# Whole-tile transfers for the residual, the result and x1's transposed copy in a one-core transformer layer

## What is computed

```
x1  = x + attention(layernorm(x)) @ Wo + bo          # one head, width 256
n   = layernorm(x1)
y   = relu(n @ up)^2 @ down                          # 1024 -> 2048 -> 1024
      + ((n @ fc1) @ expert * s) @ fc2               # s: sum of the two largest gate logits of the row
out = x1 + (layernorm(y) * gamma + beta)
```

## Time and profile before

| | |
|---|---|
| median of 3 runs | 2341.21 us (2341.16 to 2341.37) |
| the profiled execution, its own time | 2336.48 us |
| its span, first to last instruction | 2334.7 us |
| TensorE busy | 99% of the span |
| DMA traffic | 578.19 MB, 248 GB/s on average |

### The profile page before, as it was taken

How to read it: one execution, slowest core, us unless ns; L and a number is a source line. 1 busy time by engine, 2 the same in 40 slices (tenths; PEclk the granted TensorE clock), 3 DMA queues, 4 the chain that set the end, 5 groups by cost and what they waited for, 6 DMA issues and landing times.

```text
span 2334.7 us, 27253 instructions
## 1 busy us (share of the span) xinstructions
PE 2308.8 (99%) x10888; PEld 1940.2 (83%) x10888; DVE 1575.8 (67%) x1758; ACT 788.9 (34%) x875; POOL 292.9 (13%) x574
## 2 busy tenths in 40 slices
PE   9999999999999999999999999999999999999997
PEld 8988987888888878888888888888888888888886
DVE  7777658887988874598763378774249877334447
ACT  4433336666555433321221231213132122123210
POOL 3111000000223200033100023210003220000002
PEclk9999999999999999999999999999999999999999
DMA  8899854432334699889996678897668999667865
GB/s 305 334 357 367 290 193 139 169 126 79 129 111 128 222 325 324 295 279 334 329 307 202 192 272 299 311 347 250 195 218 274 323 338 308 207 192 208 243 204 181
DMA packets 232271, 578.19 MB, mean 248 GB/s; under 512 B 26320, under 2 KB 80208, under 8 KB 231760
## 3 DMA queue, kind: packets, MB, share of 16 engines
q1 hardware_dynamic: 150768, 440.90, 57.7%
q10 hardware_dynamic: 81376, 135.55, 15.8%
HBM read 420.91 MB, written 151.26 MB: 245 GB/s over the span
## 4 chain that ended last, share of the span: by engine, by line
PE 87%; DVE 6%; DMA 4%; ACT 1%; POOL 1%; issue 1%; SPq 0%; ACTq 0%; DVEq 0%; POOLq 0%
PE psum L114 86%; DMA wu_s<-QR0a 2%; DMA QR0a<-in_upfc_dram 1%; PE psum L354 1%; DVE QR0a L102 1%; DVE mx L102 1%; DVE PL L102 0%; DVE st L188 0%; DVE HB L102 0%; SPq L95 0%; DVE acc L102 0%; ACT SA L99 0%; ACT ATT L99 0%; POOL rA L102 0%; DVE ZR L108 0%
## 5 line engine op out<-in xcount | busy, mean ns | idle before, releaser
L102 DVE TENSOR_TENSOR HB<-HB,psum 128x1024 f32<-128x1024 f32 x140 | 169.2, 1218 | 302.1 <-PE psum L114 302.1
L99 ACT ACTIVATE HB<-HB 128x1024 f32<-128x1024 f32 x128 | 135.8, 1061 | 334.0 <-DVE HB L102 331.9
L105 POOL TENSOR_SCALAR veA<-mvA 128x1 f32<-128x1 f32 x32 | 31.6, 987 | 1279.5 <-DVE mvA L191 1279.5
L114 PE MATMUL psum<-XS1h,WR 128*128 128x512 f32 x560 | 174.8, 390 | 2.8 <-DMA WR<-wu_s 1.6
L114 PE MATMUL psum<-XS2h,WR 128*128 128x512 f32 x560 | 174.2, 390 | 2.0 <-DVE XS2l L102 2.0
L114 PE MATMUL psum<-XS0h,WR 128*128 128x512 f32 x560 | 175.4, 390 | 0.0
L114 PE MATMUL psum<-XS3h,WR 128*128 128x512 f32 x560 | 174.0, 389 | 0.0
L114 PEld LDWEIGHTS psum<-XS1h,WR 128*128 128x128 f32 x560 | 105.1, 188 | 25.4 <-DMA WR<-wu_s 2.3
L114 PEld LDWEIGHTS psum<-XS2h,WR 128*128 128x128 f32 x560 | 105.1, 188 | 24.1 <-issue 2.4
L114 PEld LDWEIGHTS psum<-XS0h,WR 128*128 128x128 f32 x560 | 105.2, 188 | 21.7
L114 PEld LDWEIGHTS psum<-XS3h,WR 128*128 128x128 f32 x560 | 105.1, 188 | 21.7
(11 more groups left out here) (326 smaller groups left out, 5874.7 us busy)
## 6 DMA issues: line engine op xcount, KB each, us to landing
WR<-wu_s SPq DMA_DIRECT2D x280, 512.0 KB, 4.3
WR<-wd_s SPq DMA_DIRECT2D x280, 512.0 KB, 4.8
att_s<-ATT ACTq DMA_DIRECT2D x32, 516.0 KB, 3.0
RAW<-in_x_dram SPq DMA_DIRECT2D x32, 512.0 KB, 8.5
RES<-x1b_s SPq DMA_DIRECT2D x128, 128.0 KB, 5.1
out_dram<-ZR ACTq DMA_DIRECT2D x112, 128.0 KB, 4.8
xT_s<-XT SPq DMA_DIRECT2D x24, 512.0 KB, 7.3
HB<-xT_s SPq DMA_DIRECT2D x12, 1024.0 KB, 8.2
```

Of the source, the lines that this page charges most:

```text
L99: return act.put(lambda e: e.activation(o, i, f, **kw), *toks)
L102: return (q or dve).put(lambda e: e.tensor_tensor(o, a, b, op=op), *toks)
L105: return (q or dve).put(lambda e: e.tensor_scalar(o, a, s1, s2, op0=op0, op1=op1), *toks)
L114: return pe.put(lambda e: e.matmul(o, w, m, start=start, stop=stop, **kw), *toks, sig=sig)
```

## The change

Three kinds of transfer get 128 partitions each. A task `xt(g)` stores piece m = g of all 128 partitions in place of all four pieces of 32 partitions; the number of these stores stays 24, of 512 KB each. A residual tile is one load in place of four, a result tile one store in place of four, and half a tile of the last block one store in place of four (the first half on ACT, the second on SP). ZR becomes [128, 4 tiles, 2 halves, 512], so that the halves of a result row lie side by side and a store's pieces are 4 KB in place of 2 KB. On the DRAM side each of these transfers now is a pattern of 4 blocks x 32 rows x 4 KB (2 KB in the last block).

```diff
-                src = T2[32 * g:32 * g + 32].rearrange("p m k t r -> p m (k t r)")
-                xt_st[t] = dma(xT_s[t, g].rearrange("(m c) n -> c m n", m=4), src, "xt", ln2_tr[t, 3])
+                src = T2[:, g].rearrange("p k t r -> p (k t r)")
+                xt_st[t] = dma(xT_s[t].rearrange("g (m c) n -> m g c n", m=4)[g], src, "xt", ln2_tr[t, 3])
...
-    ZR = [at("ZR0", [128, 2, 4, 512], F32, 188.125), at("ZR1", [128, 2, 4, 512], F32, 204.125)]
+    ZR = [at("ZR0", [128, 4, 2, 512], F32, 188.125), at("ZR1", [128, 4, 2, 512], F32, 204.125)]
...
-    def parts(s, r, g):
-
-        for i in range(4):
-            n = 512 * (2 * s + r) + 128 * i + 32 * g
-            yield slice(32 * i, 32 * i + 32), slice(n, n + 32)
+    def tile_rows(ap, s, r, g):
+
+        b = 512 * (2 * s + r)
+        return ap[b:b + 512].rearrange("(i g e) n -> g i e n", i=4, g=4)[g]
...
-        for ps, rs in parts(s, r, tt):
-            res_ld[s, r, tt] = dma(RES[i][ps].rearrange("p a n -> p (a n)"), x1b_s[rs], f"res{i}",
-                                   *(x1b_st[2 * s + r, q] for q in range(4)), *res_free.get(i, ()), *toks)
+        res_ld[s, r, tt] = dma(RES[i][:, :, :].rearrange("p a n -> p (a n)"), tile_rows(x1b_s, s, r, tt), f"res{i}",
+                               *(x1b_st[2 * s + r, q] for q in range(4)), *res_free.get(i, ()), *toks)
...
-        for ps, rs in parts(s, r, tt):
-            t = dma(out[rs].rearrange("p (a n) -> p a n", a=2), ZR[r][ps, :, tt, :], f"zo{r}{tt}", fin[s, r, tt], q=act)
-        z_free[r, tt] = (t,)
+        z_free[r, tt] = (dma(tile_rows(out, s, r, tt), ZR[r][:, tt].rearrange("p a n -> p (a n)"), f"zo{r}{tt}", fin[s, r, tt], q=act),)
...
-        for n, (ps, rs) in enumerate(parts(3, 1, tt)):
-            dma(out[rs, cs], ZR[1][ps, c, tt, :], f"zo{tt}{n // 2}", k, q=(act, sp)[n // 2])
+        dma(tile_rows(out, 3, 1, tt)[:, :, cs], ZR[1][:, tt, c, :], f"zo{tt}{c}", k, q=(act, sp)[c])
```

More of the change, by code:

```diff
@@ L1388, in z_evac @@
     def z_evac(s, p, ts_, b, k):
-        ZA, ZB, ZD, ZC = (ZR[r][:, c, ts_, :] for r in range(2) for c in range(2))
+        ZA, ZB, ZD, ZC = (ZR[r][:, ts_, c, :] for r in range(2) for c in range(2))
         tiles = range(ts_.start, ts_.stop)
@@ L1462, in z_stat @@
     def z_stat(s, r, tt, c):
-        bz[s, r, tt, c] = bn(ZR[r][:, c, tt, :], stz[:, tt, 6 * c:6 * c + 6], z_t[s, (("A", "B"), ("D", "C"))[r][c], tt])
+        bz[s, r, tt, c] = bn(ZR[r][:, tt, c, :], stz[:, tt, 6 * c:6 * c + 6], z_t[s, (("A", "B"), ("D", "C"))[r][c], tt])
     def z_fin(s, r, a, b):
@@ L1482, in res_load @@
         i = res_at(s, r, tt)
-        for ps, rs in parts(s, r, tt):
-            res_ld[s, r, tt] = dma(RES[i][ps].rearrange("p a n -> p (a n)"), x1b_s[rs], f"res{i}",
-                                   *(x1b_st[2 * s + r, q] for q in range(4)), *res_free.get(i, ()), *toks)
+        res_ld[s, r, tt] = dma(RES[i][:, :, :].rearrange("p a n -> p (a n)"), tile_rows(x1b_s, s, r, tt), f"res{i}",
+                               *(x1b_st[2 * s + r, q] for q in range(4)), *res_free.get(i, ()), *toks)
     gam = GAMMA[:, :].rearrange("p (a n) -> p a n", a=2)
     def z_out(s, r, tt):
-        z = ZR[r][:, :, tt, :]
+        z = ZR[r][:, tt]
         k = STT(z, z, mvZ[:, tt, 0:1], gam, ALU.subtract, ALU.mult, ag_t[s, r, tt], ld_gamma)
@@ L1668, in tail_out1 @@
     def tail_out1(tt, c):
-        z, cs = ZR[1][:, c, tt, :], slice(512 * c, 512 * c + 512)
+        z, cs = ZR[1][:, tt, c, :], slice(512 * c, 512 * c + 512)
         mul[tt] = STT(z, z, mvZ[:, tt, 0:1], GAMMA[:, cs], ALU.subtract, ALU.mult, ag_t[3, 1, tt])
     def tail_out2(tt, c):
-        z, cs = ZR[1][:, c, tt, :], slice(512 * c, 512 * c + 512)
+        z, cs = ZR[1][:, tt, c, :], slice(512 * c, 512 * c + 512)
         k = STT(z, z, rZ[:, tt:tt + 1], RES[4 + tt][:, c, :], ALU.mult, ALU.add, mul[tt], fin[3, 1, tt], res_ld[3, 1, tt])
-        for n, (ps, rs) in enumerate(parts(3, 1, tt)):
-            dma(out[rs, cs], ZR[1][ps, c, tt, :], f"zo{tt}{n // 2}", k, q=(act, sp)[n // 2])
+        dma(tile_rows(out, 3, 1, tt)[:, :, cs], ZR[1][:, tt, c, :], f"zo{tt}{c}", k, q=(act, sp)[c])
     done = {}
```

## The result

The changed kernel takes 2557.65 us (median of 4 runs, 2551.3 to 2561.9) against 2341.29 us before (4 runs). The ratio is 1.0923, with a 95% interval of 1.091 to 1.0937: it is slower by 216 us. The prediction was 2521 us, slower, with a range of 2380 to 2640. The profiled execution took 2554.63 us, its span 2552.8 us.

A forecast was written before the change was run, and what follows sets the result against it. TensorE, busy 99%, was taken to bound the kernel, with DMA hidden. Stage ends 159, first copies 12 and last block 8 made 179 us over 2336.5, 2516; plus 4.7 for the median, 2521 us, range 2380 to 2640.

The forecast's parts named there:

- The sum: Whole kernel: 159 + 12 + 8 = 179 us over the profiled execution's 2336.5 us.
- The ends of the stages: Three stretches where all changed transfers meet: four engines run late, 53 us of TensorE's time each, 159 in all.
- first copies: Copies of the other three blocks, 1050 to 1070 us and alike: 4 us each, bounds 0 and 9, 12 in all.
- stage 3: Residual loads every four chunks, 10.9 us, fill 10.7 with the weights: nothing, and 4 us in all at 20.9 GB/s.
- last block: Final result stores, 64 KB on each of four engines, nothing to hide them: 8 us more, 12 at 20.9 GB/s.
- The bound and the first step: TensorE busy 99% bounds the kernel; 4 outer blocks put each new transfer on four engines, not 16.
- slack of 9.3 us: How much later than an undisturbed landing weight pieces may come before TensorE stops; subtracted from the four engines' lateness.
- Fewer issues: SP and ACT queues: 204 issues less of 1365, costed at nothing because TensorE waits for neither.
- ZR's layout: `z_evac` sums on DVE over two runs of 512: nothing, 0.3 us if DVE did not wait for TensorE.
- Even load: Rival: all 16 engines loaded as evenly as before, not slower, 2339.7 to 2341.7 us; chance 0.11.
- the stores give way: Rival: four engines, but SP's ring is served first and ACT's stores drain behind; 2379 us, chance 0.11.
- Faster: Rival: wider transfers take over 4.7 us out of the time; 2335 us, chance 0.03.

The follow-up runs named there:

- e1_contig: Changed kernel with each new transfer's DRAM side one block of 128 rows that lie together, not 4 blocks of 32: 2338.05 us, ratio 0.9992.
- e5_halves: Changed kernel with each new transfer cut into two of 64 partitions, 2 blocks of 32 rows each: 2978.94 us, ratio 1.2725.
- e11_spread: Changed kernel with residual loads, additions and result stores of stages 0 to 2 spread, one tile every eight chunks: 2461.91 us, ratio 1.0502.
- e2_copies: Changed kernel with only the 24 copies of x1 in the new form, residual and result back to 32-partition pieces: 2417.95 us, ratio 1.0326.
- e4_result: Changed kernel with only the 36 result stores in the new form, copies and residual back to 32-partition pieces: 2389.61 us, ratio 1.0206.
- e3_residual: Changed kernel with only the 32 residual loads in the new form, copies and result back to 32-partition pieces: 2415.47 us, ratio 1.0318.
- e10_loads: Changed kernel with copies and residual loads in the new form, the result's stores back to four pieces: 2489.71 us, ratio 1.0636.
- e6_layout: Changed kernel with only ZR's new layout kept, all transfers as before with 32 partitions each: 2342.17 us, ratio 1.0003.
- e8_warm: Changed kernel with idle matmuls (6 and 2 a place) ahead of the chunks that wait for weights: 2639.4 us, ratio 1.1276.

## Why the prediction was right

**The sum: 179 us forecast, 218 measured in the profiled execution.** The mechanism and most of the size were right. The ends of the stages came out to 4 us, in part by luck, as said below. Of the rest, 19 us are missing in the first copies, 8 in stage 3 and 6 in the last block; 2 come from before them.

**The bound and the first step: right.** 21952 packets under 512 B were named for four completions, 23056 for 16; 21952 came, and 23056 in e1_contig, whose time is that of before. That transfers are dealt out by the slowest dimension is shown by e1_contig and e5_halves together. That the number is 4 rests on the completions and on the DMA share while nothing but such transfers moves: 0.26 with four blocks, 0.13 with two. Which of the 16 they are, no row shows.

**The ends of the stages: 159 us forecast, 163 measured, but made up differently.** The forecast was 53 us of waiting each. Measured are some 40 us of waiting (39.7, 40.4 and 41.4 in 1130 to 1330, 1560 to 1780 and 2010 to 2240 us) and some 14 us more in matmuls at the lower clock. So the sum with 24.5 GB/s and a slack of 9.3 us overstated the waits by a third, and the step that was missing, the lower clock, made up for it: that 159 and 163 lie so close is luck. The price itself was near, as four engines alone moved 25.5 GB/s each. The single kinds show where the formula is weak: for the copies alone, four engines have (31.45 - 2.10) / 16 + 2.10 / 4 = 2.36 MB, 96 us of work in 98, so a mean over 98 us sees no loss, and some 14 us were lost at each end. A piece that comes behind a burst of four transfers waits for that burst, whatever the mean is; e11_spread, which thins the bursts of residual and result and leaves the bytes, took 96 us off.

**The first copies: 12 us forecast, 31 measured.** This is the term that was mis-sized most, outside its bounds of 0 to 9 each. 6.1, 7.0 and 7.4 us of the 10 to 11 are waits, in three pieces each, of up to 3.6 us. In e2_copies, the same burst of four copies costs some 11 here and some 14 at an end, where the engines are full for longer (0.94 over 110 us, 0.97 over 20 here). If most of the 9.3 us of slack is not there in a stretch whose DMA share is 0.97, 13 us of backlog leave about that; this is argued, no run tries it.

**Stage 3: 0 forecast with 4 as its bound, 8.4 measured;** residual load and weights left four engines 0.2 us of 10.9, which was too little. **The last block: 8 forecast, 13.7 measured.** Its last stores take the 8 (25.0 against 17.0 us). The other 5.6 are in no term of the prediction: the last weight pieces come late behind the stores of the block before. e4_result, with the stores alone, has such 6.7 us; e2_copies, e3_residual and e10_loads, without them, have none. **Fewer issues and ZR's layout: nothing,** as e1_contig (fewer issues) and e6_layout (the layout) confirm.

**The rivals.** Even load would have shown 23056 packets. For it the Trainium skill ("SBUF — State Buffer", section "Door 1: The DMA port swizzle") was named, by which 128 partitions reach more ports than 32; when the load is even, in e1_contig, the ratio is 0.9992 (0.9982 to 1.0001), so at most 0.2% of it reaches this kernel's time. That the stores give way falls with e4_result and e10_loads. Its 2379 us left out the first copies, which stand on SP's ring in that case too: with their 12 us it is 2391. Faster was excluded already by PE's 1.0 us.

**What would show it.** PE's waits were to be about 170 us, nearly all within the three ends, and are 151.7, of which 121.5 lie there; SP's wait for the copy was to be some 20 us and is 12; the residual was to land in over 10 us, and DVE waits up to 12.8 us for it. A landing time of the new transfers is not in the DMA view: it gives none for transfers with fewer than 16 completions.

**What stays open.** The lower clock's own price (e8_warm failed to separate it), why a store costs half of a load's price when alone and more with the others, and whether the single kinds' higher price is a lower rate per engine (about 20.8 GB/s fits e3_residual) or the loss of slack in bursts. Where four engines are alone at work they are not slower than 24.5 GB/s, but no row shows their rate in the full stretch.

## What to carry to other kernels

Count the outer dimension on both sides of a DMA before making it wider: a pattern of 4 blocks x 32 rows ran on four engines and cost 1.4 to 3.2 us a transfer, by kind, though it had 128 partitions and a quarter of the issues. An average DMA share of 0.6 next to landings that took 17.8 us in place of 6.8 meant uneven engines here, not spare bandwidth; a window in which only such transfers move shows how many engines they use. When the engine that sets the time waits 1 us for DMA in all, a better transfer can win little more than that, and a worse one can lose hundreds.

## What the runs showed of the hardware that was not expected

- The time does not follow the width: with 32 partitions a transfer the kernel took 2341 us, with 64 in 2 blocks 2979, with 128 in 4 blocks 2558, with 128 joined 2338.
- Matmuls behind waits of 7 to 9 us took 0.63 us in place of 0.40 for several us; behind one of 1.87 us they did not, and behind one of 1.68 us at the kernel's end they did. Over the whole kernel matmuls took 59 us more, beside 152 us of waits.
- A moving operand read in runs of 32 columns made a matmul of 512 columns take 396 to 400 ns in place of 389 to 390.
- Reads of ACT and DVE in such runs, by halves, cost DVE 9 us in all (1584.7 against 1575.8 us busy) and ACT 11 (799.8 against 788.9), and no time at the end.
- Stores on two rings, by ACT and SP, with 4 blocks each, moved 102 GB/s together at a DMA share of 0.26; with 2 blocks each, 51 GB/s at 0.13.
